# Closing part of a fused transformer layer: TensorE turns the last block's rows, the second MoE's weights lie where K was, and the router's table moves into the general path

## The chip, the cores and the metric

One Trainium2 chip, 8 cores, all running the same program. Each core takes one sequence of 2048 tokens with 1024 features; the cores exchange nothing. The metric is the time on the device in microseconds of the slowest core, as a median over runs.

## The reference

A "macaron" layer, on x of shape 8 x 2048 x 1024:

```
x = x + 0.5 * moe(layernorm(x))
x = x + block(layernorm(x))
x = x + 0.5 * moe(layernorm(x))

moe(x):   shared = relu(x @ Ws1)^2 @ Ws2            # 1024 -> 512 -> 1024
          logits = x @ Wr; the two largest, softmax over them -> rw
          prob = trunc(rw placed at the two experts) # 8 experts
          return shared + sum_e prob[e] * (relu(x @ W1[e])^2 @ W2[e])
block(t): q, k, v = t @ Wq, t @ Wk, t @ Wv           # 16 heads of 64
          S = (q.k - 0.01 * |i - j|), masked where key index < head index, / 8
          x = layernorm(t + softmax(S) @ v @ Wo) * g1 + b1
          y = relu(x @ W1 + b1) @ W2 + b2            # 1024 -> 4096 -> 1024
          return layernorm(y + x) * g2 + b2
```

prob is truncated to whole numbers. A softmax weight over two values is below 1 unless one of them has all of it, so the routed experts count only if some token has a weight that rounds to 1. The kernel computes a flag for that (the largest of the truncated weights of all tokens) and branches: with the flag at zero the routed experts are skipped. With this input they are.

## The kernel before, in words

The work of a core is a list of steps for each engine, written out by a Python program in one order (class Seg: on() for an operation, dma() for a transfer, each with the tokens that it waits for). Every engine runs its own steps in the order in which they were emitted; waiting is by semaphores. TensorE, VectorE, ScalarE, GpSimd and SP (which issues nearly all transfers) each have such a queue. So what stands ahead of a step on its own engine holds it up, whether it depends on it or not.

Segment a (to about 158 us) is the first MoE with the value projection. Its rows are turned by TensorE (turn, L454) and moved out of PSUM by VectorE (out1, L464). Then each engine waits for the first flag and branches (branch, L1331 on). Segment b is everything else. Its main loop walks over 4 blocks of 512 query rows (tb), 8 head pairs and 16 key tiles: scores, an exponential on ScalarE (L819), a product with the distance table on VectorE (L825), and the product with V. In between, two generators are asked for steps: post_fill gives TensorE work of the block before (output projection with Wo, then W1, W2 and the shared part of the second MoE), and post_rows gives the row work (norms) on VectorE and ScalarE. The block index of both is b.

For b = 3 there is no attention left to run beside. The function drain runs the two generators to their end: it takes one step of post_fill at a time, and one of post_rows after every fourth count or when post_fill has none. These are the last 172 us, and the order in which the steps come out of drain is the order in each engine's queue.

For each block the row work and the matmuls go like this. A row tile is 128 tokens by 1024, four to a block.
- Wo: 8 matmuls and one for the bias, per half tile; VectorE adds the result into Y (L1025).
- First norm: statistics on VectorE (ln_stats, L224 to L227), two small steps on ScalarE (ln_rs, L233 and L235), a product on VectorE (L915), and the normed row in bf16 into a staging buffer SG (L922). A DMA transposes it into HT (L924, issued at L66), where the features lie on the partitions, as the next matmul wants it.
- W1 (L1052): groups of 8 matmuls and a relu on ScalarE (L1058). The first three of the eight pieces of W1 run first for tiles 0 and 1 (256 tokens wide), then for tiles 2 and 3; the rest 512 wide. W2 (L1076) follows each half of W1, its result added into Y by VectorE (L1085).
- Second norm and the norm ahead of the MoE: VectorE (L955, L956, L968, L978, L979), then ln3_out: two small steps, one more (L990) and the normed row into SG on ScalarE (L992), and again a DMA that transposes it into HT (L994).
- Second MoE (from L1100 on): 4 groups of 8 matmuls with Ws1, a relu on ScalarE (L1112) and a square on VectorE (L1114) for each; the router's logits (L1122, copied at L1127); 4 matmuls with Ws2 per half tile (L1139), added into Y and sent out (moe_out, L1162). For b = 3 it runs for tiles 0 and 1 together, then tile 2, then tile 3.
- After tile 3: the router on VectorE (L260 to L275), the flag (router_flag, L290), and four more operations, table (L278 to L281), that make the table of weights that only the general path reads.

Weights come through a ring of four 1 MB slots, RG. chunk_list names the 21 pieces of a block in order, and each ring_load issues the next one, waiting for the matmul that frees its slot. Ws1 and Ws2 (names s1, s2, from wcS1 and wcS2) are the last two pieces of a block; in b = 3 their slots are freed by the fourth row tile of the second half of W2.

At the end every engine waits for the second flag, loads it, and branches over the body of the general path, segment e2 (experts).

## Time and profile before

| | |
|---|---|
| time, three runs | 1418.31 median, 1418.12 and 1552.58 us |
| profiled execution | 1416.82 us |
| its span on the slowest core (core 1) | 1415.0 us |
| spans of the eight cores | 1403.4 to 1415.0 us |
| granted TensorE clock, mean per core | 0.982 to 0.990 |
| TensorE matmul busy | 1288.8 us, 91% of the span |
| VectorE busy | 788.6 us, 56% |
| ScalarE busy | 836.9 us, 59% |
| share of TensorE in the chain that ended last | 75% |

A span is the time from the first to the last instruction of a core; the execution's own time is 1.8 us longer. All times in rows are microseconds from the start of the span of core 1. A granted clock of 1.00 is 2.4 GHz, 0.50 is 1.2 GHz. TensorE matmuls and small helpers all carry the line of a helper (L243), so they are told apart by their operands: PS<-HT,RG reads the turned rows and a ring slot.

### The profile page before, as it was taken

The page shows a single profiled execution, that of the slowest core. Times are in us where ns is not written, and L with a number is a line of the kernel's source. Part 1 is how long each engine was busy: PE and PEld are TensorE (multiplying, and loading weights), DVE is VectorE, ACT ScalarE, POOL GpSimd, SP SyncE. Part 2 cuts the span into 40 slices and gives each one's busy share as a digit, 9 for nine tenths or more (in the row PEclk, how much of TensorE's full clock was granted, in tenths as well). Part 3 has the DMA queues.
Part 4 walks back from the last instruction along what each step waited for, and adds up shares of the span by engine and source line. Part 5 has one row for each costly group of instructions (what it writes and reads, how often), then busy time and mean ns, then how long its engine had stood idle before and what let it go on. Part 6 is the DMA issues. An engine that isn't in the chain of part 4 may idle for free.

```text
span 1415.0 us, 20648 instructions; the slowest of 8 cores (1403.4 to 1415.0 us)
## 1 busy us (share of the span) xinstructions
PE 1288.8 (91%) x6612; PEld 618.1 (44%) x6612; DVE 788.6 (56%) x1279; ACT 836.9 (59%) x1177; POOL 37.7 (3%) x67
## 2 busy tenths in 40 slices
PE   3889899999889999999899999989999999889995
PEld 2444344444334644444355444444544444445443
DVE  5865045455468544369584443885834438773146
ACT  4755477777655756767567567674665766613122
POOL 1010100000000000000000000000000000000000
PEclk9999999999999999999999999999999999999999
DMA  9957699999943412216634222165431222677435
GB/s 230 242 162 169 110 123 122 135 120 117 120 142 106 150 58 99 94 49 176 209 103 141 93 94 84 53 186 192 131 123 64 100 91 68 173 244 216 157 89 173
DMA packets 116223, 187.65 MB, mean 133 GB/s; under 512 B 55934, under 2 KB 93828, under 8 KB 105224
## 3 DMA queue, kind: packets, MB, share of 16 engines
q1 hardware_dynamic: 87688, 156.77, 35.8%
q0 software_dynamic: 28416, 29.41, 17.9%
q8 instruction: 60, 0.98, 0.3%
q14 instruction: 59, 0.48, 0.1%
HBM read 178.86 MB, written 45.09 MB: 158 GB/s over the span
## 4 chain that ended last, share of the span: by engine, by line
PE 75%; DVE 9%; ACT 6%; issue 6%; DMA 3%; SPq 0%; DVEq 0%; ACTq 0%
PE PS L243 75%; ACT EB L819 2%; DVE AT L859 1%; DMA HT<-SG 1%; DVE sm L224 1%; DVE EB L825 1%; DMA VV<-x 1%; DVE sm L226 1%; ACT RT L855 1%; ACT RT L853 1%; ACT RT L856 1%; ACT H L1058 1%; DVE Y L1162 0%; DVE Y L1025 0%; DMA RG<-wcS 0%
## 5 line engine op out<-in xcount | busy, mean ns | idle before, releaser
L819 ACT ACTIVATE EB<-PS 128x1024 bf16<-128x1024 f32 x512 | 521.6, 1023 | 316.8 <-PE PS L243 312.0
L825 DVE TENSOR_TENSOR EB<-EB,DP 128x1024 bf16<-128x1024 bf16 x512 | 352.2, 690 | 415.1 <-ACT EB L819 413.2
L243 PE MATMUL PS<-RG,H 128*128 128x512 bf16 x1280 | 313.5, 383 | 29.9 <-DVE H L1114 8.6
L243 PE MATMUL PS<-EB,VV 128*128 128x512 bf16 x1024 | 307.6, 382 | 13.0 <-DVE AT L859 9.4
L243 PE MATMUL PS<-QP,KT 128*128 128x512 bf16 x1024 | 307.6, 382 | 4.5 <-ACT EB L819 2.8
L243 PE MATMUL PS<-HT,RG 128*128 128x256 bf16 (+2 forms) x1696 | 285.6, 314 | 24.5 <-ACT H L1058 11.7
L243 PEld LDWEIGHTS PS<-HT,RG 128*128 128x128 bf16 x1696 | 164.2, 99 | 133.2 <-issue 31.0
L243 PEld LDWEIGHTS PS<-RG,H 128*128 128x128 bf16 x1280 | 124.6, 99 | 187.2 <-issue 45.1
L243 PEld LDWEIGHTS PS<-QP,KT 128*128 128x128 bf16 x1024 | 100.2, 98 | 129.1 <-issue 11.7
L243 PEld LDWEIGHTS PS<-EB,VV 128*128 128x128 bf16 x1024 | 97.3, 98 | 128.1 <-issue 36.1
L1058 ACT ACTIVATE H<-PS,sm 128x256 bf16<-128x256 f32 (+1 forms) x176 | 98.6, 570 | 75.3 <-PE PS L243 75.2
L1085 DVE TENSOR_TENSOR Y<-PS,Y 128x512 f32<-128x512 f32 x64 | 44.0, 688 | 68.2 <-PE PS L243 67.6
L859 DVE TENSOR_TENSOR AT<-PS,RT 64x512 bf16<-64x512 f32 x64 | 44.1, 689 | 41.5 <-ACT RT L856 38.8
L243 PE MATMUL PS<-RG,AT 128*128 128x512 bf16 x256 | 65.1, 380 | 1.0 <-DVE Y L1162 0.7
L243 PE MATMUL PS<-Y,RG 128*128 128x512 bf16 x192 | 52.0, 385 | 7.4 <-DVE SG L732 5.6
L243 PE MATMUL PS<-H,RG 128*128 128x512 bf16 x192 | 51.6, 390 | 5.9 <-issue 5.9
L233 ACT ACTIVATE sm<-sm 128x1 f32<-128x1 f32 x80 | 15.8, 198 | 69.3 <-DVE sm L227 34.8
L640 ACT ACTIVATE VV<-PS 128x512 bf16<-128x512 f32 x32 | 19.1, 596 | 33.4 <-PE PS L243 33.4
L243 PE MATMUL PS<-KT,VV 128*128 128x512 bf16 x128 | 32.7, 401 | 5.5 <-DVE sm L224 2.9
L243 PEld LDWEIGHTS PS<-RG,AT 128*128 128x128 bf16 x256 | 23.2, 97 | 32.0 <-issue 7.6
L224 DVE BATCH_NORM_STATS2 sm<-Y 128x6 f32<-128x512 f32 x48 | 33.1, 689 | 2.7 <-DVE Y L1025 0.9
L226 DVE BATCH_NORM_STATS2 sm<-Y 128x6 f32<-128x512 f32 x48 | 32.6, 679 | 0.0
(126 smaller groups left out, 809.3 us busy)
## 6 DMA issues: line engine op xcount, KB each, us to landing
RG<-wcW SPq DMA_DIRECT2D x64, 1024.0 KB, 5.4
RG<-wcWo SPq DMA_DIRECT2D x8, 1024.0 KB, 10.8
wcW<-W1a POOLq DMA_DIRECT2D x8, 1024.0 KB, 20.0
wcW<-W2a POOLq DMA_DIRECT2D x8, 1024.0 KB, 19.1
Y<-x1sp SPq DMA_DIRECT2D x16, 512.0 KB, 5.7
RG<-wcS SPq DMA_DIRECT2D x8, 1024.0 KB, 5.7
out<-Y SPq DMA_DIRECT2D x16, 512.0 KB, 3.2
XT<-x1sp SPq DMA_DIRECT2D x12, 512.0 KB, 4.1
```

The lines of the kernel that those rows point to most:

```text
L224: s.on("vector", lambda e: e.bn_stats(b[:, 0:6], src[:, 0:512]), wait=list(wait) + [self.bns_done[k]])
L226: t = s.on("vector", lambda e: e.bn_stats(b[:, 6:12], src[:, 512:1024]))
L233: t = s.on("scalar", lambda e: e.activation(tmp, mv[:, 1:2], AF.Ln, bias=LN_EPS, scale=1.0), wait=list(wait) + [self.tok_consts])
L243: return s.on("tensor", lambda e: e.matmul(out, lhsT, rhs, start=first, stop=last, skip_group_check=True), wait=wait, inc=inc)
L640: t = s.on("scalar", lambda e, dst=dst, src=src: e.activation(dst, src, AF.Identity, bias=0.0, scale=1.0), wait=[tm] + list(free))
L819: te = s.on("scalar", lambda e: e.activation(eb, po, AF.Exp, bias=-12.0, scale=1.0), wait=[tm, self.e_free[k], self.tok_consts])
L825: self.tok_p[k] = s.on("vector", lambda e: e.tensor_tensor(eb3, eb3, dp, ALU.mult), wait=[te, self.tok_dp])
L853: s.on("scalar", lambda e: e.activation(RT[0:64, :], a[64:128, :], AF.Ln, bias=1e-30, scale=1.0), wait=[tm, self.tok_rtfree])
L855: t = s.on("scalar", lambda e: e.activation(RT[64:128, :], b[0:64, :], AF.Ln, bias=1e-30, scale=1.0))
L859: tv = s.on("vector", lambda e, lo=lo, ps=ps: e.tensor_tensor(self.AT[lo:lo + 64, 512 * p:512 * p + 512], ps[lo:lo + 64, :], RT[lo:lo + 64 ...
L1058: th = s.on("scalar", lambda e, g=g, ps=ps, hf=hf: e.activation(hf, ps, AF.Relu, bias=self.b1c[:, g:g + 1], scale=1.0), wait=[tm, self.tok ...
L1085: t = s.on("vector", lambda e, yh=yh, ps=ps: e.tensor_add(yh, ps, yh), wait=[tm, self.tok(("fin", b))])
```

## The change

For the last block alone, the two norms write their bf16 rows not into the staging buffer SG but into VV, which holds the attention's values until then. A new function, turned, makes TensorE transpose such a row tile (two PSUM banks of four 128x128 blocks) and ScalarE move each bank into HT. It is called in post_fill directly ahead of the matmuls that read the tiles: for tiles 0 and 1, and 2 and 3, ahead of W1; for tiles 0 and 1, 2, and 3 ahead of Ws1. The DMA transposes of this block go.

The last block's Ws1 and Ws2 are no longer in the ring's list. Two transfers at the start of post_fill for b = 3 bring them into the upper half of KT, waiting only for the last matmul that read K.

The four operations of the table behind the second router are not emitted in segment b but at the head of segment e2, the general path. The first router's are emitted where they were, by the same function.

```diff
@@ router
-        def table():
-            v(lambda e: e.tensor_tensor(PR3, LT3, bc(self.v2), ALU.is_ge))
...
-            v(lambda e: e.tensor_add(self.PR, self.PR, self.eq1))
+        def table(seg, t):
+            t = seg.on("vector", lambda e: e.tensor_tensor(PR3, LT3, bc(self.v2), ALU.is_ge), wait=[t])
...
+            return seg.on("vector", lambda e: e.tensor_add(self.PR, self.PR, self.eq1), wait=[t])
@@ phase_a
-                table_pr()
+                table_pr(s, tflag)
@@ chunk_list
-            out += [(("s1", tb), self.wcS1, "s1"), (("s2", tb), self.wcS2, "s2")]
+            if tb < 3:
+                out += [(("s1", tb), self.wcS1, "s1"), (("s2", tb), self.wcS2, "s2")]
@@ post_rows, first norm
+            if b == 3:
+                sg = self.VV[:, D * tt:D * tt + D]
+                tx = s.on("vector", lambda e, tt=tt, rs=c[2], sg=sg: e.scalar_tensor_tensor(
+                    sg, Y[tt], rs, ga[:, D:2 * D], ALU.mult, ALU.add), wait=[trs, t, self.tok(("at", 3))])
+                self.put(("xt1", b, tt), tx)
+                yield 1.28
+                continue
@@ ln3_out
+        if b == 3:
+            sg = self.VV[:, 4 * D + D * tt:4 * D + D * tt + D]
+            t = s.on("scalar", lambda e: e.activation(sg, y, AF.Identity, bias=nm, scale=rs),
+                     wait=[t, self.tok(("at", 3))])
+            self.put(("xn3", b, tt), t)
+            return
@@ new
+    def turned(self, s, sg, tt, wait):
+        toks = []
+        for hh in range(2):
+            bk = self.fill_bank()
+            ps = self.bank(bk).bitcast(BF16)[:, 0:512]
+            for j in range(4):
+                c = 512 * hh + 128 * j
+                tm = s.on("tensor", lambda e, c=c, j=j, ps=ps: e.transpose(
+                    ps[:, 128 * j:128 * j + 128], sg[:, c:c + 128], self.id[:, :]),
+                    wait=[wait, self.bank_free[bk]] if j == 0 else (), inc=j == 3)
+            dst = self.HT[:, 2048 * hh:2048 * hh + 2048].rearrange("p (c t) -> p c t", c=4)[:, :, 128 * tt:128 * tt + 128]
+            src = ps.rearrange("p (c t) -> p c t", c=4)
+            t = s.on("scalar", lambda e, dst=dst, src=src: e.activation(dst, src, AF.Identity, bias=0.0, scale=1.0),
+                     wait=[tm] + self.ht_left)
+            self.bank_free[bk] = t
+            toks.append(t)
+        return toks
@@ post_fill
         yield from self.need(("at", b), 4)
+        if b == 3:
+            self.ht_left = self.ht_free
+            s1k, s2k = self.KT[:, 8192:12288], self.KT[:, 12288:16384]
+            ts1 = s.dma("sync", "ks1", s1k, self.wcS1, wait=[self.q_used[31], self.tok_wc["s1"]])
+            ts2 = s.dma("sync", "ks2", s2k, self.wcS2, wait=[self.q_used[31], self.tok_wc["s2"]])
@@ post_fill, ahead of W1
-                    tr = [self.tok(("xt1", b, tt)) for tt in range(last + 1)]
+                    if b < 3:
+                        tr = [self.tok(("xt1", b, tt)) for tt in range(last + 1)]
+                    elif fg == 0:
+                        tr = []
+                        for tt in range(lo // 128, last + 1):
+                            tr += self.turned(s, self.VV[:, D * tt:D * tt + D], tt, self.tok(("xt1", b, tt)))
@@ post_fill, second MoE
-        k1, ts1 = pieces[("s1", b)]
...
+        else:
+            self.ht_left = [self.tok_ffn1]
...
+            if b == 3:
+                tr = tr3 = tr3 + [t for tt in range(lo, hi) for t in self.turned(
+                    s, self.VV[:, 4 * D + D * tt:4 * D + D * tt + D], tt, self.tok(("xn3", b, tt)))]
@@ post_fill, after the last tile
-                table()
+                self.table2 = table
@@ build
-        self.experts(G2, self.xnT1, self.out_d, None)
+        self.experts(G2, self.xnT1, self.out_d, None, self.table2(G2, None))
```

## Rows read from the trace of the kernel before

**Rows 1.** The page's first line.

```profile
span 1415.0 us, 20648 instructions; the slowest of 8 cores (1403.4 to 1415.0 us)
```

**Rows 2.** Who TensorE waited for, 1243 to 1415: total us, times, longest.

```profile
PE PS L243 <- DMA HT<-SG: 5.9, 2, 3.8
PE PS L243 <- DMA RG<-wcS: 3.9, 1, 3.9
```

**Rows 3.** The chain that ended last, closing part: start us, us, what.

```profile
1259.22 4.91 DMA HT<-SG
...
1382.26 5.14 DMA RG<-wcS
```

**Rows 4.** Timeline, TensorE: start, us, operation, count [idle before <-releaser].

```profile
1264.26 13.33 PE L243 MATMUL PS<-HT,RG 128*128 128x256 bf16 x96 [3.84 <-DMA HT<-SG]
...
1279.70 19.21 PE L243 MATMUL PS<-HT,RG 128*128 128x256 bf16 x128 [2.11 <-DMA HT<-SG]
...
1387.86 3.65 PE L243 MATMUL PS<-HT,RG 128*128 128x256 bf16 x32 [3.88 <-DMA RG<-wcS]
...
1397.27 1.95 PE L243 MATMUL PS<-HT,RG 128*128 128x128 bf16 x32
...
1401.79 1.95 PE L243 MATMUL PS<-HT,RG 128*128 128x128 bf16 x32
```

**Rows 5.** Stretches, TensorE alone: length, busy (count), granted clock, DMA share, GB/s; last: core 2.

```profile
1264.00:1269.00 5.00, 4.74 (x23) 0.50 0.82 295
...
1282.00:1283.00 1.00, 1.00 (x7) 0.50 1.13 451
...
1376.00:1400.00 24.00, 17.54 (x145) 0.86 0.49 157
```

**Rows 6.** Timeline of transposes, then ScalarE groups by shape (busy us, mean ns | idle).

```profile
11.40 1.01 PE L454 MATMUL PS<-ids,SG 128*128 128x128 bf16 x8 [11.40 <-ACT sm L233]
...
24.53 1.01 PE L454 MATMUL PS<-ids,EB 128*128 128x128 bf16 x8 [5.78 <-DVE sm L227]
...
51.45 0.61 PE L454 MATMUL PS<-ids,EB 128*128 128x128 bf16 x8
...
L640 ACT ACTIVATE VV<-PS 128x512 bf16<-128x512 f32 x32 | 19.1, 596 | 33.4 <-PE PS L243 33.4
...
L1112 ACT ACTIVATE H<-PS 128x256 bf16<-128x256 f32 x28 | 10.7, 382 | 5.5 <-PE PS L243 5.4
```

**Rows 7.** Timeline, ScalarE and VectorE in the closing part.

```profile
1261.70 0.20 ACT L235 ACTIVATE sm<-sm 128x1 f32<-128x1 f32 x1
...
1277.69 0.48 ACT L1058 ACTIVATE H<-PS,sm 128x256 bf16<-128x256 f32 x1 [0.40 <-PE PS L243]
...
1385.73 0.15 DVE L979 TENSOR_SCALAR sm<-sm 128x1 f32<-128x1 f32 x1
1385.83 0.69 DVE L1085 TENSOR_TENSOR Y<-PS,Y 128x512 f32<-128x512 f32 x1
...
1387.29 1.24 ACT L992 ACTIVATE SG<-Y,sm 128x1024 bf16<-128x1024 f32 x1 [0.43 <-ACT sm L990]
...
1395.79 0.14 DVE L979 TENSOR_SCALAR sm<-sm 128x1 f32<-128x1 f32 x1
...
1397.07 1.24 ACT L992 ACTIVATE SG<-Y,sm 128x1024 bf16<-128x1024 f32 x1
```

**Rows 8.** Sequencer instructions behind the second flag: duration ns (three times), start us.

```profile
L1336 PEldq COMPARE_BRANCH  x1: 4017/4017/4017, 1410.6 to 1410.6; - x1
...
L1327 DVEq DRAIN  x1: 29/29/29, 1414.5 to 1414.5; - x1
L1327 PEldq DRAIN  x1: 25/25/25, 1414.7 to 1414.7; - x1
```

**Rows 9.** SP's timeline, and a stretch (engines' busy time, granted clock, DMA share, GB/s).

```profile
1262.15 0.93 SPq L68 DMA_DIRECT2D RG<-wcW  x2
...
1243.00:1264.00 21.00, 17.25 (x72) 6.35 (x72) 19.18 (x29) 1.23 (x6) 0.00 (x0) 0.98 0.73 220
```

More of the change, by code:

```diff
@@ L275, in router @@
         t = v(lambda e: e.tensor_reduce(fm, self.rden, AX.X, ALU.max))
-        def table():
-            v(lambda e: e.tensor_tensor(PR3, LT3, bc(self.v2), ALU.is_ge))
-            v(lambda e: e.tensor_tensor(PR3, PR3, bc(self.rw), ALU.mult))
-            v(lambda e: e.tensor_tensor(eq3, eq3, bc(self.rp1), ALU.mult))
-            v(lambda e: e.tensor_add(self.PR, self.PR, self.eq1))
+        def table(seg, t):
+            t = seg.on("vector", lambda e: e.tensor_tensor(PR3, LT3, bc(self.v2), ALU.is_ge), wait=[t])
+            t = seg.on("vector", lambda e: e.tensor_tensor(PR3, PR3, bc(self.rw), ALU.mult), wait=[t])
+            t = seg.on("vector", lambda e: e.tensor_tensor(eq3, eq3, bc(self.rp1), ALU.mult), wait=[t])
+            return seg.on("vector", lambda e: e.tensor_add(self.PR, self.PR, self.eq1), wait=[t])
         return t, table
@@ L290, in router_flag, with experts @@
         return s.on("vector", lambda e: e.tensor_copy(self.flag[:, k:k + 1], ps[0:1, 0:1]), wait=[tm])
-    def experts(self, s, xnT, rows_d, after_tile):
+    def experts(self, s, xnT, rows_d, after_tile, t_table=None):
         w1 = self.VV[:, 0:4096].rearrange("p (c f) -> p c f", c=8)
@@ L302, in experts @@
         bank_free = [None] * 8
-        row_st = None
+        row_st = t_table
         for tb in range(4):
@@ L1090, in post_fill @@
             tdown = tm
-        k1, ts1 = pieces[("s1", b)]
-        k2, ts2 = pieces[("s2", b)]
-        w1 = as8(self.slot(k1))
-        w2 = self.slot(k2).rearrange("p (c f) -> p c f", c=4)
+        if b < 3:
+            k1, ts1 = pieces[("s1", b)]
+            k2, ts2 = pieces[("s2", b)]
+            s1k, s2k = self.slot(k1), self.slot(k2)
+        else:
+            self.ht_left = [self.tok_ffn1]
+        w1 = as8(s1k)
+        w2 = s2k.rearrange("p (c f) -> p c f", c=4)
         wr = as8(self.wr[:, 0:64])
         hs = self.H1[:, 0:2048]
+        tr3 = []
         for lo, hi in ((0, 2), (2, 4)) if b < 3 else ((0, 2), (2, 3), (3, 4)):
```

## The prediction

> **What bounds the kernel now.** I read the views in this order. The head of the page gives the span and the spread of the cores [rows 1]. The change touches only what is emitted for the last block of 512 rows (b = 3) and for the router behind it, so everything before about 1243 us of the 1415.0 us stays as it is, and the question is what happens in the last 172 us. In the table of who waited for whom, restricted to TensorE and those 172 us, two waits concern the change: 5.9 us in two places for the rows that the DMA transposes into HT, and 3.9 us in one place for the second MoE's first weights [rows 2]. The chain of waits has the same transfers on it [rows 3]: they lie on the path that sets the end. The timeline of TensorE shows where it resumes: 1264.26 (after 3.84 idle), 1279.70 (after 2.11 idle), 1387.86 (after 3.88 idle), and, with no idle time in front of them, 1397.27 and 1401.79 for the third and fourth row tile of the second MoE [rows 4]. The granted clock stands at its 1.2 GHz level (0.50) behind the first two gaps [rows 5]. So 9.8 us of waits are on offer, and it looks as if the change took them. What decides is what takes their place.
>
> **The new operation.** A turned tile of 128 rows is 8 transposes on TensorE, then 2 moves of 128x512 from PSUM into HT on ScalarE, and nothing of it is started early: the call stands directly in front of the matmuls that need it. 8 transposes took 0.61 us at full clock and 1.01 early in the kernel [rows 6]. No row moves 128x512 bf16 out of PSUM on ScalarE; the nearest is the value projection's Identity to bf16 from f32, 0.596 us. From below the bound is 0.38, which a 128x256 move took, if a bf16 source went at double rate. I take 0.60, since the form is otherwise the same, so 2.4 us for two tiles, and 0.1 from its end to the first matmul for the release. Over the 16 moves the low bound would give back up to 3 us.
>
> **Where these moves stand in ScalarE's queue.** This decides the sum. ScalarE runs in the order of emission, and the closing loop emits TensorE's part first and one step of the row work after every fourth count of it. I place each move by its neighbours.
> Place A, the first two tiles before W1. The statistics of tile 2 (its two ScalarE steps) are already emitted, and the last ends at 1261.90 [rows 7]. TensorE is free at 1260.42 and its 16 transposes take 1.2, so they are done in time. Moves: 1261.9 + 2.4 + 0.1 = 1264.4, against 1264.26 before. **+0.15.** The DMA's 4.91 us are gone, and ScalarE gives the same time.
> Place B, tiles 2 and 3. These are normed long before, but their transposes stand behind the 12 half-width groups of W1. TensorE leaves those at 1277.59 (1264.26 + 13.33), and ScalarE ends the last relu at 1278.17 [rows 4, 7]. With the 0.15: 1278.3 + 2.4 + 0.1 = 1280.8 against 1279.70. **+0.95, in all +1.1.** The 2.11 idle is exchanged for 1.2 of transposes and about 2 idle.
> From there TensorE runs without a gap to the end of W2, at 1383.98 (1387.86 less 3.88), now 1385.1. VectorE's norm chain hangs on it and moves by 1.1 as well.
> Place C, the first two tiles of the second MoE. The weights in KT have been there for 120 us, so the 3.9 us wait is gone. But on VectorE the step of tile 2's second norm at 1385.73 stands ahead of the last add of W2 at 1385.83 [rows 7]; so its ScalarE part, ending in the 1.24 us row output at 1387.29, is emitted before the second MoE begins, and the four moves queue behind it. That output waited 0.3 for its staging buffer, which goes; it ends at 1387.0 + 1.24 + 1.1 = 1389.35. Then 2.4 + 0.1: 1391.85 against 1387.86. **+2.9, in all +4.0.** TensorE idles 5.5 us where it idled 3.88. VectorE has the square of the first hidden piece ahead of tile 3's statistics, so tile 3 is held up by all 4.0.
> Place D, tile 2. Tile 3's step at 1395.79 stands among the adds of the first two tiles, so its row output at 1397.07 is again emitted ahead of tile 2's moves [rows 7]. It ends at 1398.31 + 4.0 = 1402.3; two moves and the release make 1403.6, where TensorE used to start at 1397.27. **+2.35, in all +6.35.**
> Place E, tile 3. Its 8 transposes stand behind tile 2's down projection, after which TensorE used to go on at 1401.79 with no gap. Now 0.4 until the first bank is full, 1.2 for two moves and 0.1: **+1.7, in all +8.05.** What follows (squares, logits, down, router, flag) is unchanged in length.
>
> **The clock.** TensorE resumes after 3.84 idle at a granted clock of 0.50, and the 96 matmuls of 128x256 take 13.33 us; at full clock a relu of 0.48 comes 0.40 after the last, so 8 of them take 0.87 and 96 would take 10.4: this low stretch costs 2.9. Behind the second gap it costs 1.9 (19.21 against 10.4 for 96 and 6.9 for 32 of twice the width) [rows 4, 5, 7]. A and B keep gaps of about the old length, so both losses stay. At C core 1 was still at full clock after 3.88 idle, while core 2 averaged 0.86 over 1376 to 1400. After 5.5 idle I expect the 1.2 GHz level on most cores: the 3.65 us of the first 32 matmuls become about 6.9, of which VectorE's own work between the squares hides 1.3. I take +2.0, with 0 and +5 (another such stretch at D and E) as ends.
> Transposes alone don't seem to raise the level: a group of 8 took 1.01 at 11.40 and still 1.01 at 24.53, and 0.61 at 51.45, among matmuls [rows 6]. The Trainium skill, page "TensorE: Matmul & The Clock Gate", section "Part 4: PE-mode transpose", says that a transpose does not count as TensorE being busy in the way a matmul does and does not bring the full clock. By that rule the gap at B would be 3.1 and the one at C 6.7, and the sum would have one more low stretch of 1.9 than mine; the trace agrees as far as it goes.
>
> **The rest.** The four VectorE operations of the table behind the flag go: 1.4 us on VectorE. But TensorE's own branch over the body of the general path takes 4.02 us, and its drain is at 1414.7, VectorE's at 1414.5 [rows 8]. The cover is TensorE's branch, so I credit 0.1; without it the table would have been worth 1.4. The table of the first router is emitted where it was.
> SP loses eight DMA transposes, and so issues W1's second and third piece at 1260.5 instead of 1262.15 [rows 9]. It gains two 1 MB loads, emitted just behind W1's first piece (about 1254.5). They add 2 MB to a stretch that ran at 220 GB/s, while 451 was reached elsewhere [rows 5, 9]. W1's second piece is needed around 1270: with Y's last tile, W1's first piece and the two new ones that is 4.5 MB in some 16 us, 275 GB/s. I count nothing, with 0 and +4 as ends. The store of xn3 still lands before the branch ends.
>
> **Sum.** +8.05 + 2.0 - 0.1 = +9.95. The profiled execution took 1416.82 (span 1415.0 and 1.8 around it), which gives 1426.8. It lies 1.5 below the median of the three runs, so against that median it would be 1428.3. I say 1427.5, 0.65% slower. For this kernel about 2%, 28 us, is what a measurement can tell from no change.
>
> **Rivals.**
> 1. *Not slower: the moves pass through as soon as TensorE has turned the tiles.* Place: A and C to D. It decides if ScalarE starts them within some 0.6 us of the transposes. Then A gives -0.95, B ends at -0.15, C at -1.1 (1383.8 + 0.4 + 2.5 = 1386.7), D at +0.65, E at +2.4, and with shorter gaps the two low stretches (4.75) may go: 1418.3 + 2.4 - 4.7 = 1416. For it: the 9.8 us of waits. Against: the neighbours in the queue named above. 0.10.
> 2. *The clock rule in full.* Transposes as idle time, low stretches at B, C and D: 2 to 5 us more, 1430 to 1433. 0.14.
> 3. *The early weights collide.* 2 MB beside Y's last tile and W1's pieces: on VectorE tile 2's statistics stand behind the first use of that tile of Y, and on ScalarE the moves of A behind those statistics. +3 to +6: 1431 to 1434. Against: one queue, and the new loads stand behind the needed ones. 0.07.
> 4. *The table counts after all* (TensorE's branch is shortened by less traffic, or other cores end by VectorE): -1.4 and small gains, 1424 to 1426, within the forecast's own range. 0.05.
> 5. *Over 2% slower*: nothing in the rows adds 28 us. 0.01, and 0.01 for a gain of over 2%, which would need three times all waits on offer.
> The forecast itself has 0.62, and 1423 to 1432. The range reaches to rival 1 below and to 2 and 3 above: 1416 to 1436. Within 2%: 0.98.
>
> **What would show it.** In the changed profile: TensorE waits on ScalarE's HT where it waited for HT<-SG and RG<-wcS. A: W1 starts within 0.5 of 1264.4. B: second half at 1280.8. C: the 1.24 us row output of tile 2 stands directly ahead of four moves of about 0.6, and TensorE is idle for 5 to 6 us. D: the same with tile 3's output and two moves. E: a gap of about 1 us. The end: TensorE's drain is last, VectorE's 1.4 earlier. I am wrong if the moves are not behind the norm outputs, if they take 0.4, or if the gap at C is under 3 us.

## The result: 0.85% slower, and the profile after

The changed kernel took 1428.92 us in the median of 9 runs, against 1418.31 for the kernel before in 9 runs on the same chip. Two executions of each nine (1457 and 1643 us here, 1553 and 1614 before) fell in a slow state that is not the kernel's doing, and the ratio goes by the others: 1.0085, with a 95% interval of 1.0069 to 1.010, so slower, and within 2%. Between the two medians it is 0.75%. The prediction was 1427.5 us with a range of 1416 to 1436, and 0.98 for "within 2%".

The profiled execution of the changed kernel took 1427.38 us. The first line of its page, to hold against [rows 1]:

```profile
span 1423.4 us, 20789 instructions; the slowest of 8 cores (1415.9 to 1423.4 us)
```

**Who TensorE waited for**, changed kernel, core 7, from 1243 us to the end (total us, times, longest); the answer to [rows 2]:

```profile
PE PS L243 <- ACT HT L1031: 12.7, 5, 5.4
...
PE PS L243 <- DMA RG<-wcW: 2.6, 1, 2.6
```

The 9.8 us of waits on HT<-SG and RG<-wcS are gone. In their place stand five waits on ScalarE, which moves the turned rows from PSUM to HT, and a wait for a weight piece of W1.

**The chain that ended last**, changed kernel, closing part (start us, us, what); the answer to [rows 3]:

```profile
1258.17 11.53 DMA RG<-wcW
...
1388.05 2.05 ACT HT L1031 x4
...
1402.52 1.07 ACT HT L1031 x2
```

**TensorE's timeline**, changed kernel, core 7 (start, us, operation, count, [idle before <-releaser]); the answer to [rows 4]. L1026 is a transpose on TensorE.

```profile
1257.98 1.07 PE L1026 MATMUL PS<-ids,VV 128*128 128x128 bf16 x16
1261.95 5.32 PE L243 MATMUL PS<-HT,RG 128*128 128x256 bf16 x32 [2.90 <-ACT HT L1031]
1269.84 8.81 PE L243 MATMUL PS<-HT,RG 128*128 128x256 bf16 x64 [2.57 <-DMA RG<-wcW]
1278.49 1.06 PE L1026 MATMUL PS<-ids,VV 128*128 128x128 bf16 x16
1281.32 17.55 PE L243 MATMUL PS<-HT,RG 128*128 128x256 bf16 x128 [1.77 <-ACT HT L1031]
...
1390.23 6.56 PE L243 MATMUL PS<-HT,KT 128*128 128x256 bf16 x32 [5.41 <-ACT HT L1031]
...
1403.72 1.95 PE L243 MATMUL PS<-HT,KT 128*128 128x128 bf16 x32 [1.48 <-ACT HT L1031]
...
1409.95 1.95 PE L243 MATMUL PS<-HT,KT 128*128 128x128 bf16 x32 [1.10 <-ACT HT L1031]
```

These five gaps, 2.90, 1.77, 5.41, 1.48 and 1.10, are the same on all eight cores. They are the places A to E of the prediction.

**ScalarE and VectorE** of the same core (same columns); the answer to [rows 7]. L1002 is the row output of a norm, L1031 the move:

```profile
1259.32 0.20 ACT L235 ACTIVATE sm<-sm 128x1 f32<-128x1 f32 x1
1259.74 2.06 ACT L1031 ACTIVATE HT<-PS 128x512 bf16<-128x512 bf16 x4 [0.22 <-issue]
...
1385.68 0.15 DVE L988 TENSOR_SCALAR sm<-sm 128x1 f32<-128x1 f32 x1
1385.78 0.69 DVE L1129 TENSOR_TENSOR Y<-PS,Y 128x512 f32<-128x512 f32 x1
1386.90 1.24 ACT L1002 ACTIVATE VV<-Y,sm 128x1024 bf16<-128x1024 f32 x1
1388.05 2.04 ACT L1031 ACTIVATE HT<-PS 128x512 bf16<-128x512 bf16 x4
...
1401.37 1.24 ACT L1002 ACTIVATE VV<-Y,sm 128x1024 bf16<-128x1024 f32 x1
1402.52 1.06 ACT L1031 ACTIVATE HT<-PS 128x512 bf16<-128x512 bf16 x2
```

At C the tiles are turned and in PSUM at 1384.8 (1390.23 less 5.41), but the four moves start at 1388.05, directly behind the 1.24 us output of tile 2; at D the same with tile 3's output. A move takes 0.52 us (2.06 for four).

**SP's timeline**, same core; the answer to [rows 9]:

```profile
1252.84 1.58 SPq L68 DMA_DIRECT2D KT<-wcS  x2
...
1258.17 16.35 SPq L68 DMA_DIRECT2D RG<-wcW  x3
```

The two early 1 MB loads into KT are issued ahead of W1's second piece.

**The sequencers behind the second flag**, same core (duration ns three times, start us); the answer to [rows 8]:

```profile
L1388 DVEq COMPARE_BRANCH  x1: 63/63/63, 1418.7 to 1418.7; - x1
L1388 PEldq COMPARE_BRANCH  x1: 3319/3319/3319, 1418.8 to 1418.8; - x1
...
L1379 PEldq DRAIN  x1: 24/24/24, 1422.2 to 1422.2; - x1
...
L1379 DVEq DRAIN  x1: 23/23/23, 1422.7 to 1422.7; - x1
```

VectorE reaches its branch 0.1 us ahead of TensorE, where it was 1.0 behind it before (1411.6 against 1410.6 on core 1), as the table is gone, but its drain is not sooner against TensorE's.

**By stages.** Single cores differ by several us in when Wo ends (1254.1 to 1260.4 before, 1254.2 to 1258.8 after), where nothing was changed. So the stages are compared as means over the eight cores of the profiled execution, each from the starts and ends of TensorE's rows as shown above. "A" is from the end of Wo to the start of W1; "C" from the end of W2 to the second MoE's first matmul; the last column is from the flag matmul to the end of the span.

| kernel | A | W1 start to W2 end | C | first 32 of the MoE take | MoE start to tile 2 | tile 2 to tile 3 | tail |
|---|---|---|---|---|---|---|---|
| before | 2.63 | 117.19 | 3.89 | 5.15 | 10.49 | 4.58 | 5.39 |
| after | 3.90 | 120.38 | 6.30 | 5.37 | 12.86 | 6.23 | 5.69 |
| k_table_back | 3.90 | 120.33 | 6.31 | 5.97 | 13.23 | 6.23 | 6.70 |
| k_late_w | 3.90 | 118.31 | 6.30 | 5.63 | 13.07 | 6.23 | 5.43 |
| k_turn_only | 3.90 | 117.92 | 6.30 | 5.30 | 12.87 | 6.23 | 8.13 |
| k_dma_turn | 8.58 | 116.68 | 0.07 | 3.65 | 14.60 | 4.65 | 5.62 |
| k_dma_turn_late | 2.69 | 119.08 | 0.09 | 3.65 | 14.75 | 4.63 | 5.61 |
| k_warm_mm | 3.90 | 119.63 | 6.30 | 3.65 | 12.64 | 6.23 | 5.55 |
| k_warm_tr | 3.91 | 120.07 | 6.30 | 3.65 | 12.79 | 6.23 | 5.62 |
| k_ahead_cd_late | 3.90 | 119.44 | -0.16 | 3.66 | 13.99 | 4.63 | 5.49 |
| k_all_ahead_late | 2.16 | 117.44 | -0.16 | 3.66 | 13.94 | 4.63 | 5.68 |
| k_relu_first | 2.30 | 117.78 | -0.16 | 3.66 | 11.72 | 4.63 | 5.88 |
| k_dma_relu_first | 2.63 | 119.17 | 0.08 | 3.65 | 13.33 | 4.52 | 5.64 |
| k_vec_cde | 3.96 | 120.20 | 4.81 | 5.78 | 12.71 | 6.29 | 5.65 |

From tile 3 to the flag it is 7.88 to 7.89 everywhere. After minus before: 1.27 + 3.19 + 2.41 + 2.37 + 1.65 + 0.01 + 0.30 = 11.2 us, against 10.6 between the medians.

### The profile page after: what moved, and what is told of

The parts are those of the page before. It is cut to its first block, busy times and chain, and to the rows that moved or that the text cites. A ratio compares the mean times of both kernels' runs of the same rounds, so it can differ in the third digit from the quotient of the medians.

```text
span 1423.4 us, 20789 instructions; the slowest of 8 cores (1415.9 to 1423.4 us)
## 1 busy us (share of the span) xinstructions
PE 1294.2 (91%) x6676; PEld 622.3 (44%) x6676; DVE 787.1 (55%) x1275; ACT 843.6 (59%) x1193; POOL 37.7 (3%) x67
## 4 chain that ended last, share of the span: by engine, by line
PE 75%; DVE 8%; ACT 7%; issue 5%; DMA 3%; SPq 0%; DVEq 0%; ACTq 0%
PE PS L243 75%; ACT EB L820 2%; DVE AT L860 1%; DVE EB L826 1%; DMA VV<-x 1%; DVE sm L224 1%; DVE sm L226 1%; ACT RT L856 1%; ACT RT L854 1%; DMA RG<-wcW 1%; ACT RT L857 1%; DMA XT<-x1sp 1%; DMA HT<-SG 1%; ACT H L1102 1%; DVE Y L1214 0%
## 5 line engine op out<-in xcount | busy, mean ns | idle before, releaser
L243 PE MATMUL PS<-RG,H 128*128 128x512 bf16 x1248 | 304.9, 382 | 27.8 <-ACT H L1102 7.7
L243 PE MATMUL PS<-HT,RG 128*128 128x256 bf16 (+1 forms) x1600 | 277.4, 318 | 22.0 <-ACT H L1102 11.7
L243 PEld LDWEIGHTS PS<-HT,RG 128*128 128x128 bf16 x1600 | 156.7, 99 | 129.1 <-issue 28.3
L243 PEld LDWEIGHTS PS<-RG,H 128*128 128x128 bf16 x1248 | 121.3, 98 | 181.1 <-issue 41.5
L243 PEld LDWEIGHTS PS<-QP,KT 128*128 128x128 bf16 x1024 | 100.2, 98 | 128.7 <-issue 11.2
L224 DVE BATCH_NORM_STATS2 sm<-Y 128x6 f32<-128x512 f32 x48 | 33.1, 690 | 2.7 <-DVE Y L1064 0.9
L243 PEld LDWEIGHTS PS<-H,RG 128*128 128x128 bf16 x192 | 19.3, 101 | 30.5 <-issue 9.6
## 6 DMA issues: line engine op xcount, KB each, us to landing
RG<-wcWo SPq DMA_DIRECT2D x8, 1024.0 KB, 11.2
```

The source lines that it names most:

```text
L224: s.on("vector", lambda e: e.bn_stats(b[:, 0:6], src[:, 0:512]), wait=list(wait) + [self.bns_done[k]])
L243: return s.on("tensor", lambda e: e.matmul(out, lhsT, rhs, start=first, stop=last, skip_group_check=True), wait=wait, inc=inc)
```

## Experiments

The theory: the turning itself is cheap, and the loss is the place of the moves in ScalarE's queue, behind row outputs. The rivals: the clock after the longer gap at C, the early weights in the way of W1, the table. Where a stage of the changed kernel is compared below, the numbers are the means of the table above. Ratios are against the kernel before, on the same chip as each.

### One part undone at a time

**k_table_back**: the table's four operations stand before the second branch again.

```
-                self.table2 = table
+                table(s, tflag)
```

> The changed kernel with the four operations of the second router's table back in front of the branch, in segment b. Theory (TensorE's own branch of 4.0 us over the body of the general path hides them): the time stays that of the changed kernel, 1428.9 within 1.0 us; from the flag's matmul to the end of the span 5.2 to 6.2 us on every core, as in both kernels so far; TensorE's drain still the last or within 0.3 of VectorE's. Rival (the table was on the path): 1.4 us more, that stretch at about 7.0.

Measured: 1430.08 us, ratio 1.0074 [1.0051, 1.0098], beside 1.0085 [1.0069, 1.010] for the full change. The intervals overlap, so the time settles nothing. The tail was 6.70 us on the mean (5.8 to 7.9), 1.0 longer, where the theory had 5.2 to 6.2 and the rival 7.0; that speaks for the table counting after all, but k_turn_only below has a tail of 8.13 with no table in it, so it is not shown.

**k_late_w**: the two loads into KT are emitted after the four reloads of x1 for the row work, some 22 us later (issued 15 to 18 us after the end of Wo, where it was 5 to 7 us before it); nothing else differs.

```
 # post_fill, before W1
-            ts1 = s.dma("sync", "ks1", s1k, self.wcS1, ...)
-            ts2 = s.dma("sync", "ks2", s2k, self.wcS2, ...)
 # post_rows, b == 3, behind the loop over x1_again
+            self.ts1 = s.dma("sync", "ks1", self.KT[:, 8192:12288], self.wcS1, ...)
+            self.ts2 = s.dma("sync", "ks2", self.KT[:, 12288:16384], self.wcS2, ...)
```

> The changed kernel, but the last block's Ws1 and Ws2 are issued into KT about 25 us later, behind the reloads of x1. Theory (the two early loads stand in front of W1's second piece): TensorE's wait for RG<-wcW behind the first 32 matmuls of W1, 0.6 to 4.8 us on seven cores and 2.4 in the mean, goes to below 0.7; everything behind it unchanged, gaps at C, D, E of 5.4, 1.5, 1.1; 1426 to 1427. Rival (that wait comes from W1 starting at another moment against the other cores, not from these loads): it stays above 1.5 in the mean and the time at 1428 to 1429.

Measured: 1426.38 us, ratio 1.0054 [1.0036, 1.0071]. TensorE's wait for W1's second piece was 0.64, 3.10, 0, 3.84, 2.20, 4.80, 2.00 and 2.57 us on cores 0 to 7 of the changed kernel, 2.4 on the mean; here there is none, and the time is where the theory had it. TensorE's timeline of k_late_w, core 7:

```profile
1264.65 10.64 PE L243 MATMUL PS<-HT,RG 128*128 128x256 bf16 x96 [2.90 <-ACT HT L1033]
1275.13 1.06 PE L1028 MATMUL PS<-ids,VV 128*128 128x128 bf16 x16
1277.96 17.55 PE L243 MATMUL PS<-HT,RG 128*128 128x256 bf16 x128 [1.77 <-ACT HT L1033]
```

All 96 matmuls of W1's first three pieces on tiles 0 and 1 stand in one row, where the changed kernel has 32 and 64 with 2.57 idle between. W1 start to W2 end is 2.1 shorter. So the collision that I had priced at nothing is real and costs 2 to 2.5 us (2.1 here, 2.5 in the next run).

**k_turn_only**: TensorE turns, but the second MoE's weights come through the ring as before.

```
-            if tb < 3:
+            if True:
                 out += [(("s1", tb), ...
 # post_fill: no loads into KT; the second MoE reads pieces[("s1", b)] and pieces[("s2", b)]
```

> The changed kernel, but the last block's Ws1 and Ws2 come through the ring as before, so only the turning and the table are changed. Theory (the moves into HT queue behind ScalarE's row output, and end later than the weights land): the gap at C is still 5.4 us and its releaser ScalarE, not the transfer; no wait for W1's second piece; 1426 to 1427, so the weights in KT are worth nothing next to the turning and cost 2. Rival (the weights in KT are worth the 3.9 us of the wait that went): 1431 to 1433, TensorE waits for RG<-wcS at C.

Measured: 1426.29 us, ratio 1.0049 [1.0035, 1.0062]. Gap C is 6.30, the same as with the weights in KT: behind the 6.3 us that the turning takes, the old 3.9 us wait for the ring is hidden. The collision is gone, which is worth 2.5 us (117.92 against 120.38). This kernel has the longest tail, 8.13 us on the mean: on each core VectorE's last event comes 2.0 to 2.9 us after those of the other engines. The last events of the sequencers on its core 0 (duration ns three times, start us):

```profile
L1375 ACTq EVENT_SEMAPHORE  x1: 17/17/17, 1418.7 to 1418.7; - x1
L1375 PEldq EVENT_SEMAPHORE  x1: 51/51/51, 1418.7 to 1418.7; - x1
L1375 DVEq EVENT_SEMAPHORE  x1: 21/21/21, 1421.2 to 1421.2; - x1
```

The code of the end is the same as in the changed kernel; why these 2.5 us come is open. In the stage means they take back the 2.5 gained, so these don't account for the 3 us by which this kernel's median lies closer to the kernel before (7.4 us above it, against 10.6).

**k_dma_turn**: the DMA turns the rows as before, and the weights go early to KT.

```
 # post_rows, ahead of the staging buffer
-            if b == 3:
-                sg = self.VV[:, D * tt:D * tt + D]
...
-                continue
 # ln3_out
-        if b == 3:
-            sg = self.VV[:, 4 * D + D * tt:4 * D + D * tt + D]
...
-            return
 # post_fill, and the same in the second MoE
-                    if b < 3:
+                    if True:
                         tr = [self.tok(("xt1", b, tt)) for tt in range(last + 1)]
```

> The changed kernel, but the last block's rows go through SG and are transposed by the DMA as before, so only the weights in KT and the table are changed. Theory (the turning costs, the weights help by what the rows allow): the gap at C falls from 3.9 to 1.0 to 2.0 us, then set by HT<-SG of tile 1; no gaps at D and E; but W1's second piece is late by 2 to 3 us in the mean; 1417 to 1420. Rival (weights early are worth their whole wait): 1413 to 1415. Rival (the loss is not in the turning): above 1424.

Measured: 1425.53 us, ratio 1.0046 [1.0030, 1.0063]: a miss. The theory had 1417 to 1420, and the time is that of the last rival, "the loss is not in the turning". By the stages most of it is not the turning indeed, but the early loads. Waits of TensorE in k_dma_turn, core 1 (total us, times, longest):

```profile
PE PS L243 <- DMA HT<-SG: 7.9, 1, 7.9
...
PE PS L243 <- DVE H L1152: 5.1, 1, 5.1
```

The second is new, and the timeline of the same core shows how it comes about (TensorE, ScalarE, TensorE):

```profile
1380.01 3.65 PE L243 MATMUL PS<-HT,KT 128*128 128x256 bf16 x32
...
1383.23 1.24 ACT L993 ACTIVATE SG<-Y,sm 128x1024 bf16<-128x1024 f32 x1 [0.43 <-ACT sm L991]
1384.38 0.91 ACT L1150 ACTIVATE H<-PS 128x256 bf16<-128x256 f32 x3
...
1389.18 5.14 PE L243 MATMUL PS<-KT,H 128*128 128x512 bf16 x16 [5.13 <-DVE H L1152]
```

This is the most telling run. First, the transposes now queue on SP behind 2 MB of loads: from issue to landing the median of the first norm's four was 8.2 to 9.5 us over the cores, against 4.1 to 6.7 before, and gap A grew to 8.58. Second, gap C is gone (0.07), and yet from the end of W2 to tile 2 it takes 14.67 us against 14.38 before. **The 3.9 us wait for the weights was not on offer in this order of the queues.** Once it goes, TensorE runs ahead to the down projection and waits there 5.13 us for the squares, whose relus stand on ScalarE behind tile 2's row output. And behind that wait the granted clock is at its 1.2 GHz level: the 16 matmuls take 5.14 us here and 4.8 to 6.4 over the cores, where they took 3.61 at full clock before. So part of what the early weights give is lost to the clock.

### Is it the clock, or the queue?

**k_warm_mm**: in gap C TensorE computes 24 matmuls of 128x512 that nobody reads; **k_warm_tr**: 80 transposes that nobody reads.

```
+                if lo == 0:
+                    for _ in range(24):
+                        self.mm(s, self.bank(4), self.id[:, :], self.H1[:, 0:512], True, True)
```

```
+                if lo == 0:
+                    pt = self.bank(4).bitcast(BF16)
+                    for j in range(80):
+                        s.on("tensor", lambda e, j=j: e.transpose(
+                            pt[:, 128 * (j % 4):128 * (j % 4) + 128], self.VV[:, 4 * D:4 * D + 128], self.id[:, :]), inc=False)
```

> The changed kernel with 24 matmuls of 128x512 on data that no one reads put between the transposes of tiles 0 and 1 and the second MoE's first matmuls, in the gap of 5.4 us at C. Theory (the gap lets the clock fall, a price of its own): the first 32 matmuls with Ws1 take 3.65 us on all cores instead of 5.0 to 6.6, and since VectorE's work between the squares hides part, tile 2 starts 0.5 to 1.5 earlier against the end of W2 (19.2); 1427 to 1428. Rival (those 32 are slow for another reason, such as the weights' place in KT): they stay at 5 or more.

> The same with 80 transposes of 128x128 in place of the 24 matmuls, as long. If transposes hold the clock as matmuls do: 3.65 us for the first 32 matmuls, as in the kernel before this one in the call. If they count as idle time: 5.0 to 6.9 us, as in the changed kernel, and the granted clock at 0.50 in that stretch. By the rows of phase a (8 transposes still 1.01 us at 24.5 us) I expect the second, at 0.6 to 0.4.

Measured: 1428.24 us, 1.0072 [1.0050, 1.0094], and 1428.5 us, 1.0074 [1.0052, 1.0096]. A stretch of TensorE alone on core 7 of the changed kernel (length, busy with count, granted clock, DMA share, GB/s):

```profile
1390.00:1394.00 4.00, 3.77 (x18) 0.50 0.00 0
```

The same stretch of k_warm_mm, core 7:

```profile
1390.00:1394.00 4.00, 3.77 (x34) 1.00 0.02 4
```

After 5.41 idle, the changed kernel's first 32 matmuls start at the 1.2 GHz level and take 5.0 to 6.56 us over the cores. With gap C filled by matmuls, they run at 2.4 GHz and take 3.65 on every core. But tile 2 starts only 0.2 us earlier (12.64 against 12.86), where I had expected 0.5 to 1.5. The row of the down projection that follows shows why, first on core 7, then on core 1 of k_warm_mm:

```profile
1396.55 5.30 PE L243 MATMUL PS<-KT,H 128*128 128x512 bf16 x16 [1.92 <-DVE H L1169]
1393.47 3.61 PE L243 MATMUL PS<-KT,H 128*128 128x512 bf16 x16 [1.92 <-DVE H L1169]
```

The low stretch has not gone, it has moved: on seven cores these 16 matmuls take 5.0 to 5.3 us (granted clock 0.51 to 0.66 in the first half of the projection), where the changed kernel's take 3.6. Only on core 1 was the clock at 1.00 all through, and there tile 2 starts 11.50 us after the MoE's start. Against the mean of 12.86 in the changed kernel (12.61 to 13.49 over the cores) **the low clock costs 1.4 us there**. The kernel before paid it too: its two cores at full clock (1 and 5) took 9.41 for this stage, and the mean was 10.49, so 1.1. **What the change adds by the clock is 0.3 us, not 2.0.** The price of 1.4 rests on one core of one execution; that of 1.1 on two.

A stretch of k_warm_tr, core 7, over the end of its transposes and the matmuls behind them:

```profile
1384.00:1390.00 6.00, 5.05 (x63) 1.00 0.00 0
```

And TensorE's timeline of the same core:

```profile
1381.19 4.63 PE L1156 MATMUL PS<-ids,VV 128*128 128x128 bf16 x80
1386.76 3.65 PE L243 MATMUL PS<-HT,KT 128*128 128x256 bf16 x32 [0.94 <-ACT HT L1031]
```

Transposes back to back kept the clock as matmuls did: 3.65 us on all eight cores, and the low stretch came in the down projection as in k_warm_mm (5.0 to 5.3 us on all eight). I had given this the smaller chance, after the Trainium skill, page "TensorE: Matmul & The Clock Gate", section "Part 4: PE-mode transpose", which says that they don't count as TensorE being busy in the way matmuls do. This run disagrees with it as to keeping a clock that is already full; whether transposes alone bring it up was not tried. The rows that I had leaned on [rows 6] don't show it either: the five groups of 8 up to 25.5 us, 1.01 each, stood alone between idle times of 1.0 to 5.8 us, and the next eight matmuls of 128x512 were as slow (3.57 us at 28.44, 1.89 from 35.59 on).

**k_vec_cde**: the eight moves of the second MoE go to VectorE; ScalarE keeps those of A and B.

```
+            if self.ht_left == [self.tok_ffn1]:
+                t = s.on("vector", lambda e, dst=dst, src=src: e.tensor_copy(dst, src), wait=[tm] + self.ht_left)
```

> The changed kernel with the eight moves of the second MoE's rows on VectorE instead of ScalarE, in the same place of the order. Theory (what costs is the moves' place behind ScalarE's row output): VectorE is busy with tile 3's first statistics only, so the gap at C falls from 5.4 to 2.5 or less; the relus still wait for the row output; from the end of W2 to tile 2's first matmul 15 to 17 us instead of 19.2; 1425 to 1427. Rival (the place doesn't matter, four moves take what they take): a gap of 4.5 or more, 1428.

No ratio: there are only two times, 1432.25 and 1577.52, too few and too far apart, so it is read by its stages. Even the lower one is above the 1425 to 1427 of the theory. Timeline of VectorE and TensorE, core 0:

```profile
1391.94 0.69 DVE L1132 TENSOR_TENSOR Y<-PS,Y 128x512 f32<-128x512 f32 x1
1392.73 0.69 DVE L224 BATCH_NORM_STATS2 sm<-Y 128x6 f32<-128x512 f32 x1
1393.35 1.40 DVE L1032 COPY HT<-PS 128x512 bf16<-128x512 bf16 x4
...
1394.89 6.15 PE L243 MATMUL PS<-HT,KT 128*128 128x256 bf16 x32 [3.92 <-DVE HT L1032]
```

Back to back, a move costs 0.35 there instead of 0.52, and C fell by 1.5, from 6.30 to 4.81. The idle part was 3.92, where I had expected at most 2.5. The moves stand behind the last add of W2 and tile 3's first statistics on VectorE. At D and E nothing was gained (12.71 and 6.29, against 12.86 and 6.23): there the moves stand behind the adds of the tiles before, with TensorE idle for 1.16 us each time. From the end of W2 to tile 2 it takes 17.5 us for the expected 15 to 17, so this run is a miss and doesn't show the theory by itself; it shows another engine with the same sort of queue.

### Other places in the queues

**k_ahead_cd_late**: late weights, and each tile of the second MoE is turned one tile behind its norm: tile tt-1 just before tile tt's row output is emitted, tile 3 before tile 2's down projection.

```
 # ln3_out
+        if b == 3 and tt > 0:
+            self.turn3(s, tt - 1)
         trs = self.ln_rs(s, mv, rs, c[4], [t])
 # behind tile 2's logits
+            if b == 3 and hi == 3:
+                self.turn3(s, 3)
```

> The changed kernel with Ws1 and Ws2 issued late, and with the order of the turning changed in the second MoE alone: tiles 0, 1 and 2 are turned one tile behind the norms, so that their moves stand in ScalarE's queue ahead of the next tile's row output, and tile 3 is turned ahead of tile 2's down projection. Theory (the loss at C, D and E is the moves' place in ScalarE's queue): from the end of W2 to tile 2's first matmul 14 to 15 us instead of 19.2 (the kernel before had 14.4; the relus still stand behind tile 2's row output), from there to tile 3's 4.5 instead of 6.2; 1419 to 1421, 6 to 7 us below the changed kernel with late weights. Rival (the loss is the length of the turning, 1.1 of transposes and 2.1 of moves, wherever they stand): at least 4 of these 7 us stay, 1424 or more.

Measured: 1420.36 us, ratio 1.0012 [1.0001, 1.0024], against 1.0054 for k_late_w. It has the same transposes and moves, on the same engines and with the same lengths, and only their place differs. W2 end to tile 2 is 13.83 against 19.37, tile 2 to tile 3 4.63 against 6.23: 7.1 us in these two stages, of which 1.1 is given back between W1 and W2 (119.44 against 118.31); the medians differ by 6.0, on two chips. The clock is no part of it: in k_late_w the low stretch lies in the first 32 matmuls (5.63 on the mean for 3.66), here in the down projection (5.9 for 4.0 with its eight transposes). The forecasts came out nearly to the number: 13.83 for 14 to 15, 4.63 for 4.5, and 1420.36 for 1419 to 1421. This is the run that shows the theory.

**k_all_ahead_late**: the same for W1's tiles (turned during Wo).

```
 # after x1's row output, b == 3
+                if tt in (1, 3):
+                    self.turn1(s, tt - 1)
```

> As the kernel before this one in the call, and also ahead of W1: tile 0 is turned behind tile 1's row, tile 2 behind tile 3's, tile 3 two steps later, so only tile 1 is turned directly ahead of its matmuls. Theory: the gap at A from 2.9 to about 1.8, no gap at B and 1.1 us of transposes inside W1's first half instead of behind it; 2.5 to 3.5 us less, 1416 to 1418, at or just below the kernel before. Rival (TensorE waits inside W1 for the rows or the banks): as much is lost as is gained, 1419 to 1421.

Measured: 1418.86 us, ratio 1.0000 [0.9990, 1.0011]. A is 2.16 (I had 1.8), below the kernel before's 2.63, and there is no gap at B. The time just misses the 1416 to 1418 of the theory and stays below the rival's.

**k_dma_turn_late**: transposes by the DMA, weights late in KT (the edits of k_dma_turn and k_late_w).

```
 # beside k_dma_turn's lines
-            ts1 = s.dma("sync", "ks1", s1k, self.wcS1, ...)
+            self.ts1 = s.dma("sync", "ks1", self.KT[:, 8192:12288], self.wcS1, ...)   # behind x1_again; ks2 likewise
```

> The changed kernel with the rows transposed by the DMA as before and Ws1 and Ws2 issued into KT late: against the kernel before only the place and the moment of these weights differ (and the table). Theory (the 3.9 us wait for the second MoE's weights had ScalarE's and VectorE's queue right behind it): the wait is gone, 5 us of waiting for the squares take its place, and from the end of W2 to tile 2's first matmul it stays 14 to 15 us (before 14.4); the gap at A back at 2 to 4 us; 1417 to 1420, no different from the kernel before. Rival (the wait was on offer): 1414 to 1415.

Measured: 1423.44 us, ratio 1.0022 [1.0007, 1.0036]; the theory had 1417 to 1420. The profiled execution, at 1418.29, was the fastest of the ten, so the stages show less than the median. Waits of TensorE, core 1:

```profile
PE PS L243 <- DVE H L1153: 5.1, 1, 5.1
PE PS L243 <- DMA RG<-wcW: 3.7, 2, 2.0
```

A is back at 2.69, which shows that the early loads made the 8.58. From W2's end to tile 2 it takes 14.84 (before: 14.38). The wait for the squares stands. And TensorE now waits for weight pieces between the start of W1 and W2, 2.0 to 3.7 us over the cores, mostly ahead of W2; W1 start to W2 end is 119.08 against 117.19. That the 2 MB, moved later, delay them is argued, not shown: in k_late_w, with the same late loads, such a wait stands on two cores alone, with 0.9 and 1.0 us.

**k_relu_first**: k_all_ahead_late, and the row work of tile 2 on ScalarE is emitted behind the four relus of the first two tiles. **k_dma_relu_first**: the same order, with transposes by the DMA and late weights.

```
+            if b == 3 and tt == 2:
+                self.turn3(s, 1)
+                self.late3 = late
+                late = None
 # second MoE, behind the first four relus
+            if b == 3 and lo == 0:
+                self.ln3_out(s, b, HTt, *self.late3)
```

> As the kernel with all turning ahead and the weights late (1418.9), and tile 2's row work on ScalarE is emitted behind the four relus of tiles 0 and 1 instead of ahead of them. Theory (the squares of these tiles wait for relus that stand behind tile 2's row output): the squares come 3.5 us earlier, from the end of W2 to tile 2's first matmul 10 to 11.5 us instead of 13.8; 1415 to 1416. Rival (VectorE's own work is the bound there): 13 us or more, 1418 to 1419.

> The same reordering of ScalarE with the rows transposed by the DMA, weights in KT late, nothing turned by TensorE. Theory: the weights' early arrival now pays, since the relus no longer wait; tile 2's HT lands about 11 us after the end of W2 and sets its start, so 11 to 12.5 us instead of 14.6; 1415.5 to 1417. Rival (turning by TensorE is needed for the gain): 1418 or more.

Measured: 1417.89 us, ratio 0.9988 [0.9977, 1.0000]; the other 1420.32 us, 1.0001 [0.9987, 1.0015]. Timeline of k_relu_first, core 1, TensorE and ScalarE:

```profile
1378.29 3.66 PE L243 MATMUL PS<-HT,KT 128*128 128x256 bf16 x32
...
1379.42 0.38 ACT L1187 ACTIVATE H<-PS 128x256 bf16<-128x256 f32 x1 [1.74 <-PE PS L243]
...
1383.74 1.24 ACT L1014 ACTIVATE VV<-Y,sm 128x1024 bf16<-128x1024 f32 x1
...
1385.15 1.02 PE L243 MATMUL PS<-KT,H 128*128 128x512 bf16 x4 [2.82 <-DVE H L1189]
...
1389.04 1.95 PE L243 MATMUL PS<-HT,KT 128*128 128x128 bf16 x32
```

The relus start right behind their matmuls, 1.1 after the MoE's start where they came 4.4 after it in k_dma_turn, and the wait for the squares falls from 5.13 in k_dma_turn to 2.82. W2 end to tile 2 is 11.56, against 13.78 in k_all_ahead_late and 14.38 before. The time is 2 us above the 1415 to 1416 of the theory. On five of the eight cores the low clock stands in this down projection too; the three without it (1, 6 and 7) come to 10.6 us from the end of W2 to tile 2. k_dma_relu_first reaches only 13.41, where I had expected 11 to 12.5, and its time is the rival's: a miss. Its trace shows the step. Tile 2 waits for nothing there, so the landing of HT does not set its start; TensorE waits 3.5 to 3.9 us ahead of the down projection, for the squares on six cores, and then runs it at the 1.2 GHz level (core 1, granted clock 0.50 from 1390 to 1393):

```profile
1389.91 6.55 PE L243 MATMUL PS<-KT,H 128*128 128x512 bf16 x16 [3.46 <-DVE H L1157]
```

These 16 matmuls take 5.1 to 6.6 us over the cores, for 3.61 at full clock. k_relu_first is the best version, but its interval ends at 1.0: it equals the kernel before, or beats it by up to 0.2%. Its stages are 2.0 us shorter than before over the whole closing part (Wo's end to the end: 150.0 against 152.1).

## Why the prediction was right, and which of its terms were not

**The mechanism** was the one foretold: the waits of TensorE changed their releaser and not their place, and k_ahead_cd_late shows that the place of the moves in ScalarE's queue makes them. The predicted sum was 9.95 us, the medians differ by 10.6. It agrees better than its terms do, and that part is luck: the clock was put 1.7 too high, A 1.1 and the early weights 2.1 too low. By the stage means the 11.2 us are A 1.3, B 1.1, the early weights 2.1, C 2.4, D 2.1, the clock 0.3, E 1.65 and the tail 0.3.

**A, +0.15.** The start of W1 after the end of Wo was put at 1264.4 - 1260.42 = 3.98 and came out as 3.90 to 3.91 on every core. But the subtrahend, 3.84, was core 1's own gap [rows 4], the longest of the eight; the mean was 2.63, so the term was 1.27. Where an operation by DMA gives way to one with a fixed length, the spread over the cores goes, and the comparison must be with the mean.

**B, +0.95.** Without the collision (k_late_w) W1 start to W2 end grew by 1.12. The idle time was 1.77 for the expected 2. In this sum the low stretch behind the gap at B went: the 128 matmuls take 17.55 us on all cores, where three of the eight took 19.0 to 19.2 before [rows 4]. I had kept that loss, since the idle gap was about as long. That transposes hold the clock (k_warm_tr) may be the reason; it was not tried at B. The low stretch at A stayed, as foretold: in k_late_w its 96 matmuls take 12.0 to 13.5 us on seven cores and 10.64 on one.

**C, +2.9.** Measured 2.41. The moves took 0.52 and not 0.60, which gives back 0.3. The gap was 5.41 where 5.5 was expected.

**D, +2.35,** measured 2.37 with the clock's share of 0.3 in it, so 2.1 alone (11.50 less 9.41, both at full clock). **E, +1.7,** measured 1.65.

**The clock, +2.0,** was the mis-sized term: 0.3. The level fell as foretold (0.53 to 0.71 over the first 32 matmuls, by core), and they took 5.0 to 6.56 us instead of 3.65; I had put them at 6.9, and the mean was 5.37. Of these 1.7 us the stage shows 1.4, so little is hidden. The step that failed is the baseline: the kernel before paid 1.1 us for the same thing, since its first 32 matmuls took 5.15 on the mean. Again I had read core 1, one of two at full clock. k_warm_mm also shows that filling one gap doesn't give the loss back: the low stretch came 6 us later, behind the next wait.

**The early weights, 0, with +4 as the end.** 2 to 2.5 us by k_late_w and k_turn_only, and rival 3 held in its first half: the loads are in the way. "One queue, and the new loads stand behind the needed ones" was wrong for W1's second piece, which is issued behind them (1258.17 against 1252.84 on core 7). Its mechanism was another: they delay W1's second piece, which waits behind them on the one queue, not Y's last tile. I had set the mean rate of the stretch against the best rate seen; what counted was the order within the queue. This error and that of the clock nearly cancel.

**The table, -0.1.** TensorE's branch took 3.3 to 4.0 us over the cores (mean 3.64) instead of 3.8 to 4.4 (4.03), but on the slowest core VectorE's drain came last (1422.7) and not 1.4 earlier than TensorE's: that sign failed. The tail was not shorter (5.39, then 5.69), so the removal is worth nothing that shows. The cause of the later drain is open.

**Rival 1** fell with the gaps at C and D. Yet k_all_ahead_late, where the moves do pass at once (and the weights come late), took 1418.86 where the rival said 1416: its premise was missing, its price was near. **Rival 2**, the clock rule in full, fell with k_warm_tr at C, and at B with the 17.55 us.

## What to carry to other kernels

When work moves from a DMA queue to an engine, its price is its place in that engine's queue: the same eight moves cost 6 us more or less by which row output they were emitted behind. A wait is on offer only up to the next one: follow the chain past it (here a 3.9 us wait for weights hid a 5.1 us wait for squares, and a slow stretch of TensorE behind it) before it is counted as a gain. And a transfer started earlier "for free" is paid by whatever is issued behind it on the same queue. Read more than one core before a gap or a fast stretch is used as a baseline. And when a trial leaves the time as it was, look whether the loss has moved to the next stage before it is called small.

## What the runs showed of the hardware that was not expected

- 80 transposes of 128x128 in 4.63 us kept TensorE's granted clock at 1.00; the 32 matmuls behind them took 3.65 us on all cores.
- With gap C filled, by matmuls or by transposes, the stretch at the 1.2 GHz level came behind the next wait, of about 2 us, instead: 16 matmuls of 128x512 took 5.0 to 5.3 us on 15 of 16 cores, for 3.61 on the other.
- Moving 128x512 bf16 from PSUM to SBUF took, back to back, 0.52 us on ScalarE and 0.35 on VectorE, against 0.596 on ScalarE from an f32 source [rows 6].
- DMA transposes issued behind 2 MB of loads landed after 8.2 to 9.5 us (medians by core) instead of 4.1 to 6.7.
- The time from the last flag to the end of the span was 5.4 to 8.1 us on the mean of the cores, by program, with nearly the same code at the end.
